# The first stage of a five-stage kernel, reordered: loads by use on four semaphores, diagonals on ScalarE, normalisation in two pieces

## The chip, the cores and the metric

The kernel runs on one core of one Trainium2 chip. Its time is the device time of one execution in microseconds (us); three executions of the kernel before gave 1887.2, 1889.8 and 1894.68 us, median 1889.8. The engines are named as in the profile: PE is TensorE, DVE is VectorE, ACT is ScalarE, POOL is GpSimd, SP is SyncE, which here only issues DMAs.

## The reference, cut to what matters

Two transformer-like layers with modulation, all in float32, on x of 8 sequences of 512 tokens with 128 features. The first stage, which the change rewrites, computes what stands before the scan:

```python
mod = (_silu(L0_c) @ L0_wmod).reshape(L0_c.shape[0], 6, 1, -1)        # the same for layer 1
ga = (2 * (ga >= 0) - 1) * jnp.maximum(jnp.abs(ga), 0.25)              # the gates' bounds, 4 of them in all
h = _layernorm(x, axis=-1) * (1 + ca) + sa
x_sub = h[:, ::2]                                                      # every second token
x_sub = x_sub * jax.lax.rsqrt(jnp.mean(jnp.square(x_sub), axis=-1, keepdims=True) + EPS) * g_norm
xz = jnp.einsum('bld,ed->ble', x_sub, w_in) + b_in
x_proj, gate = jnp.split(xz, 2, axis=-1)                               # silu(gate) is applied to the scan's output
c_sum = Cm.sum(axis=0)

def step(h, xt):                                                       # 256 steps, one after the other
    h = jnp.tanh(h * A + xt[:, :, None] * Bm)
    y = h @ c_sum + Dv * xt
    return (h, y)
```

After it come the scan, an expert layer with 8 experts, attention with relative positions, and a second, routed expert layer, whose outputs are gathered token by token and added to x.

## The kernel before, in words

The program is a row of stages, each a block with one instruction stream for each engine; a stage begins when all engines have ended the one before. The first stage is `prologue`. Its tokens are laid 128 to a tile: x has 32 tiles of 128x128, and the stage needs the 16 even ones (NC). The projections take 512 tokens at a time (BLK), so there are 4 blocks (NBK).

In `prologue` before the change:

- SP issues 12 DMAs: cT, wmod, the whole of x (2 MB), then nine small ones. x counts on the semaphore x_in, the eleven others on w_in, and ACT and PE begin with a wait for all eleven (ALL_W).
- ACT takes a tanh of cT, PE forms the column sums of Cm (into csum, by DVE) and four products with wmod (mod), which ACT copies out of PSUM.
- POOL waits for csum and writes diagC with one instruction: 64 diagonal matrices of 128x128, one per state, each the identity times one column of csum. The scan's PE products take diagC as their weights. A 65th is the identity times Dv.
- DVE scales winT and woT, adds 1 to four parts of mod, bounds the four gates (four instructions each), and only then waits for x and normalises all 16 tiles: moments, root, 16 subtract-and-scale, scale, shift, square, reduce, second root, and a last product. Roots are taken by ACT (`Roots`: DVE writes the argument, ACT takes a square root, DVE refines the reciprocal).
- PE turns the 16 tiles (transposes, 4 to a PSUM bank), ACT copies each bank out (h0T), PE makes two products per block, and ACT writes xp, the raw gate and its tanh (gth) for each; DVE joins the gate's two parts.

Within an engine the order is that of the code; nothing reorders it. Between engines there are only the semaphores. In the scan that follows, each step is a chain between DVE and ACT with a length that the first stage doesn't touch. In the last stage, `experts1`, POOL gathers two rows per token tile k with indirect DMAs, counted on NGOT semaphores in turn; before those of tile k it waits until those of tile k - NGOT have landed.

Of the kernel before, what the change touches and what calls it, by code (L numbers as in the profile page):

```python
# [5 lines left out]
ALU = mybir.AluOpType  # L6
# [92 lines left out]
def layer_norm(dve, v, chain, roots, src, out, n, stats, mv, rstd, tmp, scale, shift):  # L99

    moments(v, chain, src, n, stats, mv)
    roots.rsqrt(dve, v, chain, mv[:, 0:n, 1], rstd[:, 0:n], tmp[:, 0:n])
    for k in range(n):
        chain.add(v.tensor_scalar(out[:, k, :], src[:, k, :], mv[:, k, 0:1], rstd[:, k:k + 1],
                                  ALU.subtract, ALU.mult))
    chain.wait()
    chain(v.tensor_tensor(out[:, 0:n, :], out[:, 0:n, :], scale.unsqueeze(1).to_broadcast([P, n, P]), ALU.mult))
    chain(v.tensor_tensor(out[:, 0:n, :], out[:, 0:n, :], shift.unsqueeze(1).to_broadcast([P, n, P]), ALU.add))


def prologue(nc, d, keep, scan):

    x, mod, ident, ones = keep["x"], keep["mod"], keep["ident"], keep["ones"]
    with ExitStack() as ctx:
# [31 lines left out]
        NBK = NC * P // BLK  # L146
        block = ctx.enter_context(nc.Block())

        @block.sync
        def _(sp):  # L150
            sp.dma_start(cT[:, :, :], d["cT"]).then_inc(w_in, 16)
            sp.dma_start(wmod[:, :, :], d["wmod"]).then_inc(w_in, 16)
            sp.dma_start(x[:, :, :], d["x"]).then_inc(x_in, 16)
            for dst, src in ((winT[:, :], d["w_inT"]), (binc[:, :], d["b_in"]), (gn[:, :], d["g_norm"]),
                             (cm[:, :], d["Cm"]), (am[:, :], d["A"]), (scan["Bm"][:, :], d["Bm"]),
                             (scan["Dv"][:, :], d["Dv"]), (scan["woT"][:, :], d["w_outT"]),
                             (scan["bo"][:, :], d["b_out"])):
                sp.dma_start(dst, src).then_inc(w_in, 16)

        ALL_W = 16 * 11  # L160

        @block.gpsimd
        def _(pool):
            nc.gpsimd.memset(ident[:, :], 0.0).then_inc(zero, 1)
            nc.gpsimd.memset(ones[:, :], 1.0).then_inc(id_ready, 1)
            pool.wait_ge(zero, 1)
# [10 lines left out]
            nc.gpsimd.tensor_tensor(scan["diagC"][:, NS, :], ident[:, :], scan["Dv"][:, 0:1].to_broadcast([P, P]),  # L177
                                    ALU.mult).then_inc(scan_set, 1)
            pool.wait_ge(scan_set, 3)

        @block.scalar
        def _(act):
            act.wait_ge(w_in, ALL_W)
            nc.scalar.activation(cth[:, :, :], cT[:, :, :], ACT.Tanh, scale=0.5).then_inc(c_tanh, 1)
            for n, (lo, hi) in enumerate(((0, 512), (512, 768)) * 2):
                act.wait_ge(mod_ps, n + 1)
                nc.scalar.copy(mod[:, n // 2, lo:hi], pm[n][:, 0:hi - lo]).then_inc(mod_sb, 1)
            roots.serve(act, nc, rstd[:, :], rtmp[:, :])
            roots.serve(act, nc, rstd[:, :], rtmp[:, :])
            for j in range(NBK):  # L190
                act.wait_ge(hT_ps, j + 1)
                nc.scalar.copy(hT[:, j * BLK:(j + 1) * BLK], pm[4 + j % 2][:, :]).then_inc(hT_sb, 1)
            for j in range(NBK):
                act.wait_ge(proj_ps, 2 * j + 1)
                nc.scalar.activation(scan["xp"][:, j * BLK:(j + 1) * BLK], pm[2 * (j % 2)][:, :], ACT.Identity,
                                     bias=binc[:, 0:1]).then_inc(proj_sb, 1)
# [3 lines left out]
                nc.scalar.activation(gate[:, j % 2, :], pm[2 * (j % 2) + 1][:, :], ACT.Identity,  # L200
                                     bias=binc[:, 1:2]).then_inc(proj_sb, 1)
                act.wait_ge(w_scaled, 1)
                nc.scalar.activation(gth[:, j % 2, :], pm[2 * (j % 2) + 1][:, :], ACT.Tanh,
                                     bias=binh[:, 0:1], scale=0.5).then_inc(gate_sb, 1)

        @block.vector
        def _(dve):
            v = nc.vector
            chain = Chain(dve, v_chain)
            dve.wait_ge(c_tanh, 1)  # L210

            chain(v.scalar_tensor_tensor(cth[:, :, :], cth[:, :, :], 1.0, cT[:, :, :], ALU.add, ALU.mult))
            for l in range(2):
                v.tensor_scalar(crep[:, l, :, :], cth[:, l, :].unsqueeze(1).to_broadcast([P, U, NB]), 0.5, None,
                                ALU.mult).then_inc(c_rep, 1)
            chain(v.tensor_scalar(winT[:, :], winT[:, :], gn[:, 0:1], None, ALU.mult))
# [17 lines left out]
            dve.wait_ge(x_in, 16)  # L234

            layer_norm(dve, v, chain, roots, x[:, :, :].rearrange("p (c o) e -> p c o e", o=2)[:, :, 0, :], h, NC,
                       stats, mv, rstd, rtmp, mod[:, 0, P:2 * P], mod[:, 0, 0:P])
            chain(v.tensor_tensor(sq[:, :, :], h[:, :, :], h[:, :, :], ALU.mult))
            chain(v.tensor_reduce(ms[:, :], sq[:, :, :], AX.X, ALU.add))
            chain(v.tensor_scalar(ms[:, :], ms[:, :], 1.0 / P, RMS_EPS, ALU.mult, ALU.add))  # L240
            roots.rsqrt(dve, v, chain, ms[:, :], rstd[:, :], rtmp[:, :])
            v.tensor_tensor(h[:, :, :], h[:, :, :], rstd[:, :].unsqueeze(2).to_broadcast([P, NC, P]),
                            ALU.mult).then_inc(h_ready, 1)
            for j in range(NBK):
                dve.wait_ge(gate_sb, j + 1)

                v.scalar_tensor_tensor(scan["gate"][:, j * BLK:(j + 1) * BLK], gth[:, j % 2, :], 1.0,
                                       gate[:, j % 2, :], ALU.add, ALU.mult).then_inc(gate_used, 1)

        @block.tensor  # L250
        def _(pe):
            mm = nc.tensor.matmul
            pe.wait_ge(w_in, ALL_W)
            pe.wait_ge(id_ready, 2)
# [1578 lines left out]
```

## Time and profile before

| | us |
|---|---|
| median of three executions | 1889.8 |
| lowest, highest | 1887.2, 1894.68 |
| the profiled execution's own time | 1888.83 |
| its span, first to last instruction | 1887.1 |
| first instruction of the scan stage (POOL, after the barrier) | 73.92 |
| last instruction of the first stage (DVE, the fourth gate), end | 73.60 |

The page puts PE at 79% of the span, DVE at 70%, ACT at 48%, POOL at 32%; these are means over stages of different kinds. The first stage takes 73.9 of the 1887.1 us. A row of the timeline reads: start in us, duration in us, engine, line of the code, operation, what it writes and reads, how many were merged into the row, and in brackets how long the engine sat idle before it and what released it. The granted TensorE clock was 0.874 of full speed over the span.

### The profile page before, as it was taken

What the parts mean: (1) busy time and instruction counts of PE and PEld (TensorE: products, weight loads), DVE (VectorE), ACT (ScalarE), POOL (GpSimd) and SP (SyncE); (2) the same over time, 40 slices, a digit from 0 to 9 for tenths busy, and PEclk for the clock granted to TensorE, in tenths of its full rate; (3) what the DMA queues carried; (4) which work ended last, traced back from release to release, by engine and by line L of the source; (5) the groups of instructions that cost most, each with busy time, mean ns of one, the idle gap of its engine ahead of it and who ended that gap; (6) DMA issues with size and microseconds to landing.
All of it is one profiled execution on the core that took longest, in us unless ns stands there. A gap on an engine that the chain in (4) does not pass through costs nothing. (4 is left out here: it accounts for less than half of the span.)

```text
span 1887.1 us, 41774 instructions
## 1 busy us (share of the span) xinstructions
PE 1487.2 (79%) x15118; PEld 1007.2 (53%) x15118; DVE 1326.4 (70%) x3609; ACT 908.8 (48%) x2099; POOL 612.6 (32%) x586
## 2 busy tenths in 40 slices
PE   1277777767699399999999999999999395298490
PEld 0177766766554245555555555555555363187370
DVE  6699999999559636666666666666666674177385
ACT  1455555555121226666666666666666122065250
POOL 3496666662103325111111111111110317502414
PEclk7688888888789799999999999999999777599695
DMA  1400000000000012111111111111110001258342
GB/s 68 118 12 1 1 1 1 1 1 1 12 1 1 17 17 35 28 29 29 28 29 30 29 29 30 29 30 30 30 25 8 15 1 56 65 150 224 94 135 78
DMA packets 146373, 71.54 MB, mean 38 GB/s; under 512 B 95218, under 2 KB 131588, under 8 KB 146052
## 3 DMA queue, kind: packets, MB, share of 16 engines
q1 hardware_dynamic: 141508, 60.62, 14.6%
q0 software_dynamic: 4096, 8.40, 1.5%
q8 instruction: 107, 1.75, 0.4%
q14 instruction: 86, 0.70, 0.1%
q10 hardware_dynamic: 576, 0.07, 0.0%
HBM read 38.11 MB, written 18.35 MB: 30 GB/s over the span
## 5 line engine op out<-in xcount | busy, mean ns | idle before, releaser
L1190 DVE TENSOR_REDUCE ntop<-score 128x1 f32<-128x512 f32 x512 | 318.1, 683 | 253.0 <-PE score L1071 252.9
L1149 ACT ACTIVATE prob<-score,ntop 128x512 f32<-128x512 f32 x512 | 317.6, 687 | 270.0 <-DVE ntop L1190 269.9
L391 ACT ACTIVATE hist<-zp 128x168 f32<-128x168 f32 (+1 forms) x768 | 224.1, 313 | 171.6 <-DVE zp L359 170.9
L1107 PE MATMUL turned<-ident,prob 128*128 128x128 f32 x2048 | 268.5, 280 | 1.5 <-DVE probT L1133 1.5
L441 PEld LDWEIGHTS py<-hist,diagC 128*128 128x128 f32 x2048 | 262.7, 214 | 0.0
L441 PE MATMUL py<-hist,diagC 128*128 128x128 f32 x2048 | 262.5, 297 | 0.0
L1071 PE MATMUL score<-ks,qs 64*128 64x512 f32 x1024 | 257.5, 622 | 0.0
L1107 PEld LDWEIGHTS turned<-ident,prob 128*128 128x128 f32 x2048 | 218.9, 141 | 49.4 <-issue 28.7
L411 POOL TENSOR_TENSOR xb<-xc,Bm 128x1024 f32<-128x1024 f32 x128 | 244.7, 1950 | 1.3
L354 DVE TENSOR_TENSOR gp<-hist,Ap 128x168 f32<-128x168 f32 (+1 forms) x768 | 231.0, 331 | 14.9 <-POOL xb L411 14.9
L359 DVE TENSOR_TENSOR zp<-gp,xb 128x168 f32<-128x168 f32 (+1 forms) x768 | 234.6, 336 | 0.0
L836 POOL TENSOR_TENSOR qr<-rel_q,own_shift 128x256 f32<-128x256 f32 x64 | 37.2, 613 | 549.3 <-DMA key_q<-q_sb 549.3
L1133 ACT COPY probT<-turned 128x512 f32<-128x512 f32 x384 | 198.4, 594 | 1.2 <-PE turned L1107 1.2
L1071 PEld LDWEIGHTS score<-ks,qs 64*128 64x128 f32 x1024 | 89.1, 188 | 169.0 <-issue 169.0
L1091 PEld LDWEIGHTS mixed<-probT,vh 128*16 128x16 f32 x4096 | 100.7, 96 | 95.8 <-issue 95.8
L1067 PE MATMUL score<-tb,qr 32*32 32x512 f32 x4096 | 148.1, 600 | 4.0 <-PEq L850 3.9
L1091 PE MATMUL mixed<-probT,vh 128*16 128x128 f32 x4096 | 136.4, 274 | 0.7 <-issue 0.7
L1449 POOL DMA_INDIRECT got<-sorted_y,pos x64 | 61.1, 954 | 169.3 <-DMA sorted_y<-ysb 150.4
L1177 DVE RECIPROCAL inv<-cm 128x256 f32<-128x256 f32 x64 | 111.5, 1742 | 0.0
L842 POOL TENSOR_TENSOR qs<-key_q,own_batch 128x256 f32<-128x256 f32 x128 | 95.5, 787 | 0.0
L1133 DVE COPY probT<-turned 128x512 f32<-128x512 f32 x128 | 88.5, 691 | 0.1
L1440 POOL DMA_INDIRECT sorted_h<-hz,pos x64 | 63.2, 987 | 48.9 <-DVE pos L1573 29.7
(299 smaller groups left out, 1652.8 us busy)
## 6 DMA issues: line engine op xcount, KB each, us to landing
w<-in_ew SPq DMA_DIRECT2D x46, 320.0 KB
tb<-in_table SPq DMA_DIRECT2D x64, 127.1 KB
sorted_h<-nought SPq DMA_DIRECT2D x2, 2944.0 KB, 17.1
xs<-sorted_h SPq DMA_DIRECT2D x46, 128.0 KB
sorted_y<-ysb SPq DMA_DIRECT2D x46, 128.0 KB
rel_q<-q_sb SPq DMA_DIRECT2D x256, 8.0 KB
ks<-k_sb SPq DMA_DIRECT2D x32, 128.0 KB
key_q<-q_sb SPq DMA_DIRECT2D x248, 8.0 KB
```

The lines of the kernel that those rows point to most:

```text
L354: v.tensor_tensor(g[:, lo:hi], prev[:, lo:hi], Ap[:, lo:hi], ALU.mult).then_inc(decayed, 1)
L359: v.tensor_tensor(zp[j][:, 0:hi - lo], g[:, lo:hi], xb[:, par, u, lo:hi], ALU.add)\
L391: nc.scalar.activation(hist[:, par, u, lo:hi], zp[j][:, 0:hi - lo], ACT.Tanh)\
L411: nc.gpsimd.tensor_tensor(xb[:, par, u:u + XB_STEPS, :].rearrange("p u (s b) -> p u s b", b=NB), xc[:, par, u * NB:(u + XB_STEPS) * NB].re ...
L441: last = mm(py[par][:, 0:P], diagC[:, s, :], hist[:, par, :, s * NB:(s + 1) * NB], start=False, stop=(s == NS - 1))
L1067: mm(score_ps[r][32 * w:32 * w + 32, :], qr[p][rows, w, g, :, :].rearrange("p b v -> p (b v)"), tb[p][rows, s:s + SEQ], start=True, stop=F ...
L1071: mm(score_ps[r][:, :], qs[p][rows, r % 2, g, :, :, :].rearrange("p w b v -> p (w b v)"), ks[p][rows, :], start=False, stop=True).then_inc ...
L1091: last = mm(mixed_ps[32 * c:32 * c + SUMS, bh * P:(bh + 1) * P], vh[:, p, j, b, :], probT[G // 2 % 2][:, j, :, :].rearrange("p t (w b v) - ...
L1107: last = nc.tensor.transpose(turned_ps[BANK[e]][:, j * P:(j + 1) * P], prob[G % 2][e][:, j * P:(j + 1) * P], ident[:, :])
L1133: copy(probT[G // 2 % 2][:, :, G % 2 * GRP + TURN[e], :], turned_ps[BANK[e]][:, :].rearrange("p (j t) -> p j t", j=JT))\
L1149: nc.scalar.activation(prob[G % 2][e][:, :], score_ps[r][:, :], ACT.Exp, bias=ntop[:, G % 2, e:e + 1]).then_inc(prob_ready, 1)
L1190: v.tensor_reduce(ntop[:, G % 2, e:e + 1], score_ps[r][:, :], AX.X, ALU.max, negate=True)\
```

## The change

The first stage is written in another order, and the last one counts its gathers on 4 semaphores in place of 8.

- Loads: cm and cT go first on c_in, then wmod on wmod_in, then only the even tiles of x on x_in (16 pieces of 512 bytes per partition), then the eight small ones and last the odd tiles of x on w_in.
- diagC is written by ACT with 65 instructions, each a Copy of the identity with a column of csum (or Dv) as its scale, in five groups of 12, 20, 12, 20 and 1 between its other work; POOL writes the two constants and a zero only.
- DVE begins the moments behind x_in. Normalisation after the first root goes in two pieces of 8 tiles; between them it scales winT and binh. The gates' bounds, woT and A come after the second piece and the first two joined gates.
- PE turns and projects blocks 0 and 1 behind the first piece, blocks 2 and 3 behind the second. ACT's square root for the second piece stands between its work on blocks 0 and 1.
- In `experts1` NGOT is 4.

```diff
@@ prologue, loads
+            sp.dma_start(cm[:, :], d["Cm"]).then_inc(c_in, 16)
+            sp.dma_start(cT[:, :, :], d["cT"]).then_inc(c_in, 16)
+            sp.dma_start(wmod[:, :, :], d["wmod"]).then_inc(wmod_in, 16)
+            sp.dma_start(by_use(x[:, :, :])[:, :, 0, :], by_use(d["x"])[:, :, 0, :]).then_inc(x_in, 16)
             for dst, src in ((winT[:, :], d["w_inT"]), (binc[:, :], d["b_in"]), (gn[:, :], d["g_norm"]),
...
+                             (by_use(x[:, :, :])[:, :, 1, :], by_use(d["x"])[:, :, 1, :])):
                 sp.dma_start(dst, src).then_inc(w_in, 16)
@@ gpsimd
-            nc.gpsimd.tensor_tensor(scan["diagC"][:, 0:NS, :], ident[:, :].unsqueeze(1).to_broadcast([P, NS, P]),
-                                    csum[:, :].unsqueeze(2).to_broadcast([P, NS, P]), ALU.mult).then_inc(scan_set, 1)
@@ scalar
+            def diagonals(lo, hi):
+                for s in range(lo, hi):
+                    A.activation(scan["diagC"][:, s, :], ident[:, :], ACT.Copy, scale=csum[:, s:s + 1])
...
+            act.wait_ge(c_in, 32)
+            A.activation(cth[:, :, :], cT[:, :, :], ACT.Tanh, scale=0.5).then_inc(c_tanh, 1)
+            act.wait_ge(id_ready, 3)
+            act.wait_ge(csum_sb, 1)
+            diagonals(0, 12)
+            for n, (lo, hi) in enumerate(((0, 512), (512, 768)) * 2):
+                act.wait_ge(mod_ps, n + 1)
+                A.copy(mod[:, n // 2, lo:hi], pm[n][:, 0:hi - lo]).then_inc(mod_sb, 1)
+            roots.serve(act, nc, rstd[:, :], rtmp[:, :])
+            diagonals(12, 32)
+            roots.serve(act, nc, rrms[:, 0:PER], rtmp[:, 0:PER])
+            diagonals(32, 44)
+            act.wait_ge(w_in, ALL_W)
+            for j in range(BLKS):
+                columns(j)
+            act.wait_ge(w_scaled, 1)
+            projected(0)
+            roots.serve(act, nc, rrms[:, PER:NC], rtmp[:, PER:NC])
+            projected(1)
+            for j in range(BLKS, NBK):
+                columns(j)
+            diagonals(44, NS)
+            A.activation(scan["diagC"][:, NS, :], ident[:, :], ACT.Copy, scale=scan["Dv"][:, 0:1]).then_inc(scan_set, 1)
+            for j in range(BLKS, NBK):
+                projected(j)
@@ vector
+            dve.wait_ge(x_in, 16)
+            xe = by_use(x[:, :, :])[:, :, 0, :]
+            moments(v, chain, xe, NC, stats, mv)
+            roots.rsqrt(dve, v, chain, mv[:, :, 1], rstd[:, :], rtmp[:, :])
+            dve.wait_ge(mod_sb, 1)
+            scale, shift = mod[:, 0, P:2 * P], mod[:, 0, 0:P]
+            chain(v.tensor_scalar(scale, scale, 1.0, None, ALU.add))
+            def piece(i):
+                ts = slice(i * PER, (i + 1) * PER)
+                wide = lambda t: t.unsqueeze(1).to_broadcast([P, PER, P])
+                for k in range(i * PER, (i + 1) * PER):
+                    chain.add(v.tensor_scalar(h[:, k, :], xe[:, k, :], mv[:, k, 0:1], rstd[:, k:k + 1],
+                                              ALU.subtract, ALU.mult))
+                chain.wait()
+                chain(v.tensor_tensor(h[:, ts, :], h[:, ts, :], wide(scale), ALU.mult))
+                chain(v.tensor_tensor(h[:, ts, :], h[:, ts, :], wide(shift), ALU.add))
+                chain(v.tensor_tensor(sq[:, ts, :], h[:, ts, :], h[:, ts, :], ALU.mult))
+                chain(v.tensor_reduce(ms[:, ts], sq[:, ts, :], AX.X, ALU.add))
+                chain(v.tensor_scalar(ms[:, ts], ms[:, ts], 1.0 / P, RMS_EPS, ALU.mult, ALU.add))
+                roots.rsqrt(dve, v, chain, ms[:, ts], rrms[:, ts], rtmp[:, ts])
+                v.tensor_tensor(h[:, ts, :], h[:, ts, :], rrms[:, ts].unsqueeze(2).to_broadcast([P, PER, P]),
+                                ALU.mult).then_inc(h_ready, 1)
...
+            piece(0)
+            dve.wait_ge(w_in, ALL_W)
             chain(v.tensor_scalar(winT[:, :], winT[:, :], gn[:, 0:1], None, ALU.mult))
+            v.tensor_scalar(binh[:, :], binc[:, 1:2], 0.5, None, ALU.mult).then_inc(w_scaled, 1)
+            piece(1)
+            gated(0)
+            gated(1)
             chain(v.tensor_scalar(scan["woT"][:, :], scan["woT"][:, :], 0.5, None, ALU.mult))
...
@@ tensor
+            for i in range(PIECES):
+                for j in range(i * BLKS, (i + 1) * BLKS):
+                    turned(j)
+                for j in range(i * BLKS, (i + 1) * BLKS):
+                    projected(j)
@@ experts1
-    NW, NX, NY, NGOT = 5, 4, 4, 8
+    NW, NX, NY, NGOT = 5, 4, 4, 4
```

How the orders move, in three places. First DVE, at the start of the moments (L91). Before, the last of the four gates' bounds (guard) stood ahead of them:

```order
L230 TENSOR_SCALAR guard<-mod 128x128
L231 SCALAR_TENSOR_TENSOR guard<-mod 128x128
L232 TENSOR_SCALAR guard<-guard 128x128
L233 SCALAR_TENSOR_TENSOR mod<-guard 128x128
L91 BN_STATS stats<-x 128x6 x16
L94 BN_AGGR mv<-stats 128x2 x16
L96 TENSOR_SCALAR mv<-mv 128x16
L74 TENSOR_SCALAR rtmp<-mv 128x16
```

The same engine in the changed kernel, from its first instruction that does work:

```order
L226 COPY csum<-pm 128x64
L229 SCALAR_TENSOR_TENSOR cth<-cth,cT 128x16
L231 TENSOR_SCALAR crep<-cth 128x128 x2
L91 BN_STATS stats<-x 128x6 x16
L94 BN_AGGR mv<-stats 128x2 x16
L96 TENSOR_SCALAR mv<-mv 128x16
L74 TENSOR_SCALAR rtmp<-mv 128x16
```

Of the instructions on mod, the gates, winT, woT and A none is left ahead of the moments: one (1 added to the scale) stands behind the first root, the others behind the first piece or later.

Second ACT, from the square roots (rstd, rrms) to the first two blocks' tanh (gth). Before:

```order
L85 ACT_TABLE_LOAD
L85 ACTIVATE rstd<-rtmp 128x16 x2
L192 COPY h0T<-pm 128x512 x4
L195 ACTIVATE xp<-pm,binc 128x512
L200 ACTIVATE gate<-pm,binc 128x512
L203 ACT_TABLE_LOAD
L203 ACTIVATE gth<-pm,binh 128x512
L195 ACTIVATE xp<-pm,binc 128x512
```

ACT in the changed kernel, from the third group of diagonals:

```order
L176 ACTIVATE diagC<-ident,csum 128x128 x12
L180 COPY h0T<-pm 128x512 x2
L184 ACTIVATE xp<-pm,binc 128x512
L189 ACTIVATE gate<-pm,binc 128x512
L191 ACT_TABLE_LOAD
L191 ACTIVATE gth<-pm,binh 128x512
L85 ACT_TABLE_LOAD
L85 ACTIVATE rrms<-rtmp 128x8
L184 ACTIVATE xp<-pm,binc 128x512
L189 ACTIVATE gate<-pm,binc 128x512
L191 ACT_TABLE_LOAD
L191 ACTIVATE gth<-pm,binh 128x512
```

The second piece's root now stands between two tanhs, with a table load before and after it.

Third ACT at the end of the stage. Before, the last two blocks followed one another:

```order
L195 ACTIVATE xp<-pm,binc 128x512
L200 ACTIVATE gate<-pm,binc 128x512
L203 ACTIVATE gth<-pm,binh 128x512
L195 ACTIVATE xp<-pm,binc 128x512
L200 ACTIVATE gate<-pm,binc 128x512
L203 ACTIVATE gth<-pm,binh 128x512
```

The end of the stage on ACT in the changed kernel, from the copies of blocks 2 and 3 (h0T):

```order
L180 COPY h0T<-pm 128x512 x2
L176 ACTIVATE diagC<-ident,csum 128x128 x20
L216 ACTIVATE diagC<-ident,Dv 128x128
L184 ACTIVATE xp<-pm,binc 128x512
L189 ACTIVATE gate<-pm,binc 128x512
L191 ACTIVATE gth<-pm,binh 128x512
L184 ACTIVATE xp<-pm,binc 128x512
L189 ACTIVATE gate<-pm,binc 128x512
L191 ACTIVATE gth<-pm,binh 128x512
```

21 diagonals now stand between the copies and the last two blocks.

## Rows read from the trace of the kernel before

**Rows 1.** Busy time by stretch: us, busy us (instructions) by engine, clock, DMA, GB/s.

```profile
core 0: us, PE busy (x) PEld busy (x) DVE busy (x) ACT busy (x) POOL busy (x), PEclk, DMA share, GB/s
18.30:29.10 10.80, 0.00 (x0) 0.00 (x0) 10.77 (x2) 1.26 (x1) 10.73 (x2) 0.58 0.00 0
...
34.40:58.20 23.80, 0.00 (x0) 0.00 (x0) 22.58 (x67) 0.43 (x2) 0.00 (x0) 0.50 0.00 0
```

**Rows 2.** Timeline, the load of x and the first work behind the loads.

```profile
1.74 0.43 SPq L153 DMA_DIRECT2D x<-in_x  x1
...
12.51 0.22 ACT L184 ACTIVATE cth<-cT 128x16 f32<-128x16 f32 x1 [10.41 <-DMA bo<-in_b_out]
```

**Rows 3.** DMA view: x's landing; then 6-10, 10-12.3 and 78-90 us.

```profile
x<-in_x SPq DMA_DIRECT2D x1, 2048.0 KB, 9.0
...
DMA packets 106, 1.60 MB, mean 399 GB/s; under 512 B 3, under 2 KB 9, under 8 KB 9
...
DMA packets 1161, 0.29 MB, mean 127 GB/s; under 512 B 910, under 2 KB 1161, under 8 KB 1161
...
DMA packets 6767, 3.46 MB, mean 289 GB/s; under 512 B 16, under 2 KB 6766, under 8 KB 6766
```

**Rows 4.** Timeline, 12.5 to 34.4 us: modulation, diagonals, gates' bounds.

```profile
13.39 4.40 PE L258 MATMUL pm<-wmod,crep 128*128 128x512 f32 x8 [0.17 <-DVE crep L214]
...
14.79 13.88 POOL L174 TENSOR_TENSOR diagC<-ident,csum 128x8192 f32<-128x8192 f32 x1 [12.78 <-DVE csum L222]
...
18.29 10.82 DVE L226 TENSOR_SCALAR mod<-mod 128x128 f32<-128x128 f32 x2 [3.65 <-ACT mod L187]
...
34.04 0.29 DVE L233 SCALAR_TENSOR_TENSOR mod<-guard 128x128 f32<-128x128 f32 x1
```

**Rows 5.** Timeline, 34.4 to 58.2 us: normalisation.

```profile
34.37 3.19 DVE L91 BATCH_NORM_STATS2 stats<-x 128x6 f32<-128x128 f32 x16
...
39.22 0.21 ACT L85 ACTIVATE rstd<-rtmp 128x16 f32<-128x16 f32 x1 [19.66 <-DVE rtmp L74]
...
40.59 4.19 DVE L104 TENSOR_SCALAR h<-x,mv,rstd 128x128 f32<-128x128 f32 x16
...
54.11 0.17 DVE L240 TENSOR_SCALAR ms<-ms 128x16 f32<-128x16 f32 x1
...
55.90 2.29 DVE L242 TENSOR_TENSOR h<-h,rstd 128x2048 f32<-128x2048 f32 x1
```

**Rows 6.** Timeline, 58.2 to 73.6 us: transposes, projections, gates.

```profile
58.25 3.76 PE L265 MATMUL pm<-ident,h 128*128 128x128 f32 x16 [40.46 <-DVE h L242]
...
60.26 0.58 ACT L192 COPY h0T<-pm 128x512 f32<-128x512 f32 x1 [0.27 <-PE pm L265]
...
65.70 1.28 ACT L203 ACT_TABLE_LOAD   x1
66.99 0.69 ACT L203 ACTIVATE gth<-pm,binh 128x512 f32<-128x512 f32 x1
...
69.28 0.70 ACT L195 ACTIVATE xp<-pm,binc 128x512 f32<-128x512 f32 x1
...
72.91 0.69 DVE L247 SCALAR_TENSOR_TENSOR gate<-gth,gate 128x512 f32<-128x512 f32 x1 [1.04 <-ACT gth L203]
```

**Rows 7.** Prices elsewhere: groups by form (DVE, ACT), then timeline of eight ACT.

```profile
L354 DVE TENSOR_TENSOR gp<-hist,Ap 128x168 f32<-128x168 f32 (+1 forms) x768 | 231.0, 331 | 14.9 <-POOL xb L411 14.9
...
L670 ACT COPY acc<-px 128x128 f32<-128x128 f32 x32 | 6.9, 269 | 58.3 <-PE px L742 58.3
...
1509.72 3.19 ACT L537 ACTIVATE hz<-x,offsetz,rstdz 128x128 f32<-128x128 f32 x8 [1.54 <-DVE offsetz L501]
```

**Rows 8.** End: last gather, data moved 1868 to 1872 us (40 slices), last combining.

```profile
1867.85 0.94 POOL L1449 DMA_INDIRECT got<-sorted_y,pos  x1 [0.30 <-issue]
...
GB/s 0 0 246 164 246 0 0 0 0 0 0 0 0 0 0 287 287 82 0 0 0 0 0 0 0 0 0 0 0 0 0 0 0 0 0 0 0 0 0 0
...
1880.17 3.06 DVE L1629 SCALAR_TENSOR_TENSOR acc<-got,wt,acc 128x128 f32<-128x128 f32 x8
```

More of the change, by code:

```diff
@@ L96, in moments @@
     chain(v.tensor_scalar(mv[:, 0:n, 1], mv[:, 0:n, 1], LN_EPS, None, ALU.add))
[L99 to L108, printed above, removed]
 def prologue(nc, d, keep, scan):
     x, mod, ident, ones = keep["x"], keep["mod"], keep["ident"], keep["ones"]
+    PIECES = 2
+    PER = NC // PIECES
     with ExitStack() as ctx:
@@ L185, in _ @@
[L185 to L190, printed above, removed]
+            A = nc.scalar
+            def diagonals(lo, hi):
+                for s in range(lo, hi):
+                    A.activation(scan["diagC"][:, s, :], ident[:, :], ACT.Copy, scale=csum[:, s:s + 1])
@@ L191, in _, with columns, projected @@
+            def columns(j):
                 act.wait_ge(hT_ps, j + 1)
[L192 to L193 removed]
+                A.copy(hT[:, j * BLK:(j + 1) * BLK], pm[4 + j % 2][:, :]).then_inc(hT_sb, 1)
+            def projected(j):
                 act.wait_ge(proj_ps, 2 * j + 1)
[L195 to L196 removed]
+                A.activation(scan["xp"][:, j * BLK:(j + 1) * BLK], pm[2 * (j % 2)][:, :], ACT.Identity,
+                             bias=binc[:, 0:1]).then_inc(proj_sb, 1)
@@ L199, in _ @@
                     act.wait_ge(gate_used, j - 1)
[L200 to L204, printed above, removed]
+                A.activation(gate[:, j % 2, :], pm[2 * (j % 2) + 1][:, :], ACT.Identity,
+                             bias=binc[:, 1:2]).then_inc(proj_sb, 1)
+                A.activation(gth[:, j % 2, :], pm[2 * (j % 2) + 1][:, :], ACT.Tanh,
+                             bias=binh[:, 0:1], scale=0.5).then_inc(gate_sb, 1)
+            act.wait_ge(c_in, 32)
[23 more added lines that the diff above has]
+                projected(j)
+            act.wait_ge(scan_set, 1)
         @block.vector
@@ L233, in _ @@
                     chain(v.scalar_tensor_tensor(g, guard[:, 0, :], -1.0, guard[:, 1, :], ALU.add, ALU.mult))
[L234 to L248, printed above, removed]
+            for j in range(BLKS, NBK):
+                gated(j)
         @block.tensor
@@ L252, in _, with turned @@
             mm = nc.tensor.matmul
-            pe.wait_ge(w_in, ALL_W)
-            pe.wait_ge(id_ready, 2)
-            mm(pm[7][:, 0:NS], ones[:, :], cm[:, :], start=True, stop=True).then_inc(csum_ps, 1)
-            pe.wait_ge(c_rep, 2)
-            for n, (lo, hi) in enumerate(((0, 512), (512, 768)) * 2):
-                mm(pm[n][:, 0:hi - lo], crep[:, n // 2, :, :].rearrange("p u b -> p (u b)"),
-                   wmod[:, n // 2, lo:hi], start=True, stop=True).then_inc(mod_ps, 1)
-            pe.wait_ge(h_ready, 1)
-            for j in range(NBK):
+            def turned(j):
+                pe.wait_ge(h_ready, j // BLKS + 1)
                 if j >= 2:
@@ L266, in _, with projected @@
                 last.then_inc(hT_ps, 1)
-            for j in range(NBK):
+            def projected(j):
                 pe.wait_ge(hT_sb, j + 1)
```

50 lines of the change are left out of this document (29 added, 21 removed).

## The prediction

> **What bounds the kernel now.** I read the busy time by stretch first, then the timeline of the first stage, and then only as much of the last stage as the gathers need. The code between is the same in both kernels, and the scan's first instruction waits for a barrier of all engines at 73.9 us, so the question is when the first stage's last instruction ends. Before, that is the fourth joined gate, at 72.91 + 0.69 = 73.6 us [rows 6].
>
> The stage is one chain with four parts. Nothing but DMAs runs until 12.5: ACT's first tanh is released by the last load to land [rows 2]. From 12.5 to 34.4 comes work that normalisation doesn't need, and in it the striking row: DVE's two additions on 128x128 tiles take 10.82 us, while POOL's single product for diagC runs from 14.79 to 28.67 [rows 4]. Both engines are busy for the whole stretch of 10.8 us, and DVE does two instructions in it [rows 1]. The reader is to see that a busy DVE there is a held DVE. From 34.4 to 58.2 DVE alone works (22.6 of 23.8 us) and PE nothing [rows 1]; then PE, ACT and DVE take turns until 73.6 [rows 6]. So DVE's start on the moments, at 34.37 [rows 5], hangs on all loads, on POOL and on the gates' bounds, and on nothing that the moments use: x itself landed at 1.74 + 9.0 = 10.7 [rows 2, 3].
>
> **The change, part by part.** I build the new stage forward in time from the span's start.
>
> *The even half of x.* x is 2.10 MB and in long packets moved at 399 GB/s [rows 3], so 5.3 us, which puts its start at about 5.5. Ahead of it now stands cm too, 32 KB of 256-byte rows, at 127 GB/s [rows 3] 0.3 us: 5.8. The half is 1.05 MB, but in pieces of 512 bytes. Packets of that size went at 289 GB/s in a store [rows 3]: 3.6 us, landing at 9.4. Bounds: 399 GB/s gives 8.4, and 127 GB/s, the rate of the still smaller ones, gives 14.1. I take 9.4, by the row of equal size. The odd half and the small loads follow it, by the same rates until about 16; nothing waits for them before 26.
>
> *Early ACT and PE work* costs nothing. wmod lands at about 5.5, PE's eight products take 4.4 [rows 4], so the copies of mod end near 10.3. Twelve diagonals lie ahead of those copies, in time when ACT has nothing else. The root is first asked for 4.8 us after the moments begin (34.37 to 39.22 [rows 5]), at 14.2. Slack 2.5 us and more with the table load.
>
> *Moments, root, scale:* 40.59 - 34.37 = 6.2 [rows 5], and one addition of 0.3: 15.9. POOL has no product any more, so nothing holds DVE.
>
> *A piece.* Eight subtractions are half of 4.19, 2.1. Five passes of 1024 elements: a pass of 2048 takes 2.29 [rows 5] and one of 168 takes 0.33 [rows 7], so 1024 takes 1.22, with the gap 1.26, in all 6.3. The mean and the root are 55.90 - 54.11 = 1.8 [rows 5]. Sum 10.2. The first piece ends at 26.1. In whole, two pieces are 20.4 where one pass of all 16 tiles was 17.6 (40.59 to 58.19): splitting costs 2.8 us of DVE. winT and binh I put at 0.3 each, like an instruction of the gates' bounds (0.29 [rows 4]); the second piece starts at 26.7 and, if its root is served at once, ends at 36.9.
>
> *ACT between.* 65 diagonals are new on ACT. No row shows a Copy of 128 columns with one pointer for its scale, from SBUF. A copy without one takes 0.27, and two ACTIVATEs in a row overlap: six with 0.70 each end 3.6 after the first starts [rows 6], 0.6 each, so 0.17 is the lower end. Eight of 128 columns with two pointers took 3.19 [rows 7], 0.40 each, the upper end. I take 0.29, half way. The Trainium skill (ScalarE: Activation LUTs, section What ACT_TABLE_LOAD costs) has this price: 186 ns, 0.833 ns per element and 93 ns per pointer, less 93 ns of overlap; that would be 0.293 each, an estimate by the page. Twenty lie between the roots: 14.4 to 20.2 (22.4 at 0.40), and the next root is asked for at 23.5. Twelve more end at 27.2; PE's first bank is turned at 26.1 + 1.1 (16 transposes take 3.76 with waits [rows 6]), 27.2. Level, so an ACT slower than this is late here.
>
> *The second root.* Before, the first gth began at 66.99, 8.7 after the transposes did, with four banks turned ahead of the first product [rows 6]. With two banks it is half of 3.76 less, 6.8: it ends at 26.1 + 6.8 + 0.7 = 33.6, and the next table load (1.28) at 34.9. DVE asks for the root at 26.7 + 2.1 + 4 x 1.26 + 0.4 = 34.2: with ACT's own steps 0.8 late. The second piece ends at 37.7. The Trainium skill speaks against this (ScalarE: Activation LUTs, section What ACT_TABLE_LOAD costs): it adds some 1.38 us of drain to every switch of tables, which for the two loads on this path would be 2.8 us more, an estimate by that page. The trace disagrees: gth starts 0.01 after its table load ends [rows 6]. I keep 0.8.
>
> *The end.* Transposes and copies of two banks: 60.26 + 0.58 - 58.20 = 2.6 [rows 6], 40.3. The 21 diagonals, the part that I find costly, are on the path now, for DVE waits for gates 2 and 3 only: 21 x 0.29 = 6.1 (3.6 to 8.4), 46.4. Six ACTIVATEs 3.6 and the last gate 0.7 [rows 6]: 50.7. What runs beside: DVE joins two gates by 39.5 and does what I moved there, the bounds with two additions (34.33 less 18.29 + 10.82, 5.2 [rows 4]) and 1.0 for the rest, by 46; gate 2 is asked of it at 48.2. PE's last products (eight instructions took 4.4 [rows 4]) end by 45.
>
> *NGOT 4.* A gather waits for the one 8 issues back, 8 x 1.24 = 10 us, instead of 16 back. The last gather is issued at 1867.85, the last data move at 1869.8 (the second burst, slices 15 to 17 of 0.1 us) [rows 8], 2 us. Nothing by data movement; and the last eight combinings begin at 1880.2, 11 us later, so the tail hangs on DVE. What this row can't show is when the semaphore counts: bounds 0 and the rival below.
>
> The sum: 73.6 - 50.7 = 22.9 us. On its own time, 1888.8, that gives 1865.9; the profiled execution is 1.0 below the median of the runs, so against 1889.8 it is 1866.9. I forecast 1867.
>
> **The rivals.**
>
> *ACT becomes the bound of the stage.* For it: 19 us of new work on an engine that already closes the stage. With 0.40 per diagonal the last group costs 2.3 more, the third ends 1.3 late and pushes the second root by as much: 3.6 us, 1870.5. Beside it, a mechanism of its own: ACT stands idle behind each table load for as long again as the load. Two loads stand on the path to the second root, so twice 1.3 from the row of the load, 2.6 us: 1869.5. Against it, the gap of 0.01 [rows 6]. It is the rule of the Trainium skill named above.
>
> *x comes no earlier than everything else.* 2048 short packets, or a queue that ends its 13 loads together: x_in fires at 14.1 to 15. Then everything moves by 5: 1872. For it: the slow last stretch of the loads (127 GB/s). Against it: 289 GB/s for 512 bytes.
>
> *Slower than before: the gathers' count comes late.* If a gather's semaphore is counted not 2 but L us after its issue, POOL stands still L - 10 us in each of the three rounds of the second half that wait for a gather of that half, and the last gather's own L follows: 1867.9 + 3(L - 10) + L, against 1882.5, when DVE takes the last rows now (the last two of eight from 1880.17). It eats the 22.9 from L = 16.9 on; L = 20 gives 1867.9 + 30 + 20 = 1917.9 for the last rows, 35.4 later than now, in all 1866.9 + 35.4 = 1902: 12 slower. For it: before, POOL waited only for gathers 20 us old, so an unwaited step of 0.94 + 0.30 says only that L is under 20. Against it: data done in 2 us [rows 8].
>
> **How the numbers follow.** The forecast's own case 0.77; ACT as the bound, drains included, 0.09; x late 0.08; gathers 0.03; something in the unchanged stages that moves by some us, 0.03. Below: x at 8.4 (1.0), diagonals at 0.17 (2.5), no late root (0.8) give 1862.6, and the three runs lie up to 2.6 under their median: 1859. Above: the first two rivals together, 3.6 + 5, give 1875.5: 1876. The range is 1859 to 1876. What can be told from no change is 0.5%, 9.4 us. Every case but the gathers' and part of the last is beyond it: faster 0.95, same 0.02, slower 0.03.
>
> **What would show it.** Moments beginning at 9.4 (8.4 to 14.1); POOL idle and no DVE instruction of 128x128 above 0.3 us; the first piece's last product ending at 26.1, the second's at 37.7; 65 diagonals at 0.29 a piece; the second rrms root 0.8 after DVE asks; the scan's first instruction at 51.0; gathers in steps of 1.24 with no wait between. The forecast is wrong if the scan begins after 56, or if it begins at 51 and the time is not within 5 us of 1867, which would put the cause behind the first stage.

## The result, and the profile after

| | before | changed |
|---|---|---|
| median of 4 executions each, us | 1888.5 (1883.44 to 1894.68) | 1865.47 (1855.28 to 1869.98) |
| ratio, 95% interval | | 0.9866 [0.9819, 0.9912] |
| the profiled execution's own time, span | 1888.83, 1887.1 | 1868.96, 1867.2 |
| scan stage's first instruction | 73.92 | 51.78 |

The change made the kernel 1.3% faster. The forecast was 1867, range 1859 to 1876. Between the two profiled executions lie 19.9 us, and 22.1 of them were there when the scan began. Nothing of that was given back in the scan or in attention: at the first scatter of the last stage the lead is 23.8 us. It is 17.4 at the first gather, 20.0 at the 33rd and 19.9 at the end.

The first stage of the changed kernel in the timeline; columns as in [rows 2]. First, up to the end of the first piece:

```profile
2.92 0.22 ACT L195 ACTIVATE cth<-cT 128x16 f32<-128x16 f32 x1 [0.82 <-DMA cT<-in_cT]
...
3.99 3.61 ACT L176 ACTIVATE diagC<-ident,csum 128x128 f32<-128x128 f32 x12 [0.85 <-DVE csum L226]
...
6.57 5.01 PE L318 MATMUL pm<-wmod,crep 128*128 128x512 f32 x8 [2.94 <-DMA wmod<-in_wmod]
...
9.99 3.19 DVE L91 BATCH_NORM_STATS2 stats<-x 128x6 f32<-128x128 f32 x16 [5.62 <-DMA x<-in_x]
...
14.96 5.94 ACT L176 ACTIVATE diagC<-ident,csum 128x128 f32<-128x128 f32 x20
...
16.47 2.14 DVE L246 TENSOR_SCALAR h<-x,mv,rstd 128x128 f32<-128x128 f32 x8
...
25.38 1.23 DVE L255 TENSOR_TENSOR h<-h,rrms 128x1024 f32<-128x1024 f32 x1
```

The reader is to see the bracket behind L91: DVE now waits for x alone, and starts at 9.99 where it started at 34.37 [rows 5]. ACT begins at 2.92, not 12.51 [rows 2], and no DVE row of 128x128 is a held one.

The same view, from the first piece's end to the scan:

```profile
28.57 5.12 PE L309 MATMUL pm<-h0T,winT 128*128 128x512 f32 x8
...
34.02 0.69 ACT L191 ACTIVATE gth<-pm,binh 128x512 f32<-128x512 f32 x1
...
34.38 0.17 DVE L74 TENSOR_SCALAR rtmp<-ms 128x8 f32<-128x8 f32 x1
34.72 1.28 ACT L85 ACT_TABLE_LOAD   x1
36.02 0.21 ACT L85 ACTIVATE rrms<-rtmp 128x8 f32<-128x8 f32 x1
...
36.26 0.20 DVE L76 RECIPROCAL rrms<-rrms 128x8 f32<-128x8 f32 x1 [1.71 <-ACT rrms L85]
...
37.30 1.23 DVE L255 TENSOR_TENSOR h<-h,rrms 128x1024 f32<-128x1024 f32 x1
...
41.07 5.95 ACT L176 ACTIVATE diagC<-ident,csum 128x128 f32<-128x128 f32 x20
...
46.92 0.39 ACT L216 ACTIVATE diagC<-ident,Dv 128x128 f32<-128x128 f32 x1
47.21 0.67 ACT L184 ACTIVATE xp<-pm,binc 128x512 f32<-128x512 f32 x1
...
50.77 0.69 DVE L261 SCALAR_TENSOR_TENSOR gate<-gth,gate 128x512 f32<-128x512 f32 x1 [0.96 <-ACT gth L191]
51.78 0.29 POOL L457 COPY xc<-xp 128x128 f32<-128x128 f32 x1 [49.63 <-POOLq L104]
```

Two things on ACT set the end. The second piece's root is asked for at 34.38 + 0.17 and comes at 36.02, behind the tanh and a table load, so DVE sits idle 1.71 us where a root served at once costs 0.28. And 21 diagonals hold back blocks 2 and 3 from 41.07 to 47.21.

Busy time by stretch, the view of [rows 1]:

```profile
9.90:26.70 16.80, 1.68 (x4) 0.54 (x2) 15.46 (x61) 10.81 (x34) 0.00 (x0) 0.63 0.25 68
26.70:38.50 11.80, 6.94 (x16) 3.60 (x16) 9.68 (x23) 9.37 (x15) 0.00 (x0) 0.79 0.00 1
38.50:51.50 13.00, 6.14 (x16) 3.36 (x16) 8.11 (x26) 11.61 (x31) 0.00 (x0) 0.76 0.00 0
```

DVE bounds the first stretch (15.46 of 16.80), no engine the second alone, and ACT the third (11.61 of 13.00): the bound of the stage moved from DVE to ACT.

### The profile page after: what moved, and what is told of

It reads as the page before. It is cut to its first block and busy times, and to the rows that moved or that the text cites. A ratio compares the mean times of both kernels' runs of the same rounds, so it can differ in the third digit from the quotient of the medians.

```text
span 1867.2 us, 41862 instructions
## 1 busy us (share of the span) xinstructions
PE 1491.4 (80%) x15118; PEld 1010.8 (54%) x15118; DVE 1317.8 (71%) x3621; ACT 930.6 (50%) x2167; POOL 598.7 (32%) x584
## 5 line engine op out<-in xcount | busy, mean ns | idle before, releaser
L403 DVE TENSOR_TENSOR gp<-hist,Ap 128x168 f32<-128x168 f32 (+1 forms) x768 | 231.1, 331 | 14.7 <-POOL xb L460 14.7
```

The lines of the kernel that those rows point to most:

```text
L403: v.tensor_tensor(g[:, lo:hi], prev[:, lo:hi], Ap[:, lo:hi], ALU.mult).then_inc(decayed, 1)
```

## The experiments

The scan's first instruction is the measure for edits to the first stage; why, the last section says. How far it repeats, traces of the same first stage show: the changed kernel's began the scan at 51.78, 51.79 (e5) and 51.50 (e10), the one before at 73.92 and 72.69 (e6). One execution each unless more are given. e1 to e4 ran on one chip, beside "before" at 1876.8 (one execution), e5 to e8 on a second, beside 1882.57 (median of 11, 1874.72 to 1894.3), and the last three on a third. The question of the first four was which part of the change brought what, and what POOL's product really held.

**e1, the kernel before with the gates' bounds behind normalisation.**

```diff
+            chain(v.tensor_scalar(mod[:, 0, P:2 * P], mod[:, 0, P:2 * P], 1.0, None, ALU.add))
             chain(v.tensor_scalar(winT[:, :], winT[:, :], gn[:, 0:1], None, ALU.mult))
...
+            dve.wait_ge(x_in, 16)
+            layer_norm(...)        # then woT, A, the other additions and the bounds
```

> The kernel before with one edit: DVE does only the csum copy, the scale's addition, winT and binh ahead of the moments, and the gates' bounds, woT and A behind normalisation, where DVE waits for gates anyway. Loads and POOL's diagC as before. Read: start of the scan (73.9 us before). Theory A, POOL's product holds every DVE instruction: moments begin near 28.7 instead of 34.4, the scan at 68.2. Theory B, it holds only DVE instructions of some kinds (tensor_scalar on a large tile among them) and lets the moments' instructions through: the moments begin near 17 while POOL works, the subtractions at 28.7 instead of 40.6, the scan at about 62. If the bounds don't fit into DVE's idle time, either is later by up to 5.

1872.11 us; the scan began at 66.81, 7.1 earlier than before. The timeline of this kernel:

```profile
13.32 13.88 POOL L174 TENSOR_TENSOR diagC<-ident,csum 128x8192 f32<-128x8192 f32 x1 [11.31 <-DVE csum L217]
...
15.80 11.48 DVE L219 TENSOR_SCALAR mod<-mod 128x128 f32<-128x128 f32 x1 [2.63 <-ACT mod L187]
...
27.81 3.18 DVE L91 BATCH_NORM_STATS2 stats<-x 128x6 f32<-128x128 f32 x16
```

The first addition is held until POOL ends, and the moments behind it with it. Of the 7.1 us, 1.5 come from POOL starting earlier (13.32 for 14.79 [rows 4]). The times are near those of theory A (27.8 for 28.7, 66.8 for 68.2), but that doesn't decide between the theories: whether the moments themselves would be held stayed open, since a held instruction stood in front of them.

**e2, the kernel before with the diagonals on ACT**, 30 ahead of the first root and 35 behind it.

```diff
-            nc.gpsimd.tensor_tensor(scan["diagC"][:, 0:NS, :], ...)
+            for s in range(30):
+                nc.scalar.activation(scan["diagC"][:, s, :], ident[:, :], ACT.Copy, scale=csum[:, s:s + 1])
             roots.serve(act, nc, rstd[:, :], rtmp[:, :])
+            for s in range(30, NS): ...
```

> The kernel before with one edit: the 65 diagonals by ACT, 30 ahead of the first root and 35 between the two roots, where ACT is idle; POOL's products are gone. Loads and DVE's order as before. Read: start of the scan (73.9 us before). My theory: DVE's two additions take 0.5 instead of 10.8 us, ACT's 65 x 0.30 us = 19.3 are hidden, and the scan starts at 63.6. Rival: DVE was not held by POOL but by something else at that place, and the scan stays at 73.9.

1875.77 us; the scan began at 63.38, 10.5 earlier.

```profile
18.17 0.49 DVE L228 TENSOR_SCALAR mod<-mod 128x128 f32<-128x128 f32 x2 [3.40 <-ACT mod L180]
...
23.92 3.19 DVE L91 BATCH_NORM_STATS2 stats<-x 128x6 f32<-128x128 f32 x16
```

The two additions that took 10.82 [rows 4] take 0.49. What held DVE was POOL's product and nothing else, and taking it off POOL is worth 10.5 us here, by itself.

**e3, the changed kernel with normalisation in one piece.**

```diff
-    PIECES = 2
+    PIECES = 1
```

> The changed kernel with PIECES = 1: all 16 tiles normalised in one piece, then all transposes and projections as before the change; the diagonals stay in ACT's five groups. Read: start of the scan (51.8 us in the changed kernel). My theory: two pieces cost DVE 2.8 us and a late root 1.5, and give back the transposes and products of two blocks; by the old rows 16.5 + 17.6 + 0.5 = 34.6 for the last product, 14.7 to the last gth, 6.3 for the 21 diagonals, 0.7 for the last gate: 56.3, so the scan at 56.6, 4.8 later. Rival: the split gives nothing, because what it overlaps comes back as 2.8 + 1.5 and waits: the scan within 1 us of 51.8.

1860.08 us; the scan began at 54.53, 2.8 later than in the changed kernel. I had expected 4.8.

```profile
37.58 3.62 PE L305 MATMUL pm<-h0T,winT 128*128 128x512 f32 x8
```

Of the 2.0 us missing, 0.8 is the last product of normalisation, which ended at 33.8 and not 34.6. Most of the rest is PE: its first eight products took 3.62 at a granted clock of 1.00 (2.4 GHz), where they took 5.12 at 0.72 in the changed kernel and 4.87 at 0.74 before, both of which run their first products at 0.50 (1.2 GHz). Splitting pays, though it gives DVE more work (2.8 us by the prediction's working).

**e4, the changed kernel with diagC by POOL again.**

```diff
+            pool.wait_ge(csum_sb, 1)
+            nc.gpsimd.tensor_tensor(scan["diagC"][:, 0:NS, :], ...)
@@ scalar
-            diagonals(...)          # all five groups
```

> The changed kernel with diagC by POOL again, as one product behind csum (ready at 3.9 us) and the small one for Dv behind the loads; ACT makes no diagonals. Read: start of the scan (51.8 us in the changed kernel) and what DVE does until 18. POOL's product runs from 4 to 18. Theory A, it holds every DVE instruction: the moments start at 18, 8 us late, ACT's last 21 diagonals (6.2) and its lateness (1.5) are gone: scan at 52. Theory B, the moments pass (10 to 14.6) and the subtractions wait until 18, 1.5 us late: the scan at 45.6 to 47.6, where DVE's own gates' bounds, which end at 46.2 now, are the next bound.

1864.83 us; the scan began at 58.33, 6.5 later than in the changed kernel.

```profile
4.08 14.04 DVE L232 TENSOR_SCALAR crep<-cth 128x128 f32<-128x128 f32 x2
4.12 13.92 POOL L169 TENSOR_TENSOR diagC<-ident,csum 128x8192 f32<-128x8192 f32 x1 [1.97 <-DVE csum L227]
...
18.05 1.05 DVE L91 BATCH_NORM_STATS2 stats<-x 128x6 f32<-128x128 f32 x5
...
18.18 1.22 PE L319 MATMUL pm<-wmod,crep 128*128 128x512 f32 x1 [14.47 <-DVE crep L232]
```

Neither theory's time came out, because the product caught crep, which both had forgotten: PE waited for it until 18.18, and mod with it. The experiment was badly placed; e9 mends it.

**e9, the same with csum copied behind crep**, so that POOL starts after it.

```diff
-            dve.wait_ge(csum_ps, 1)
-            v.tensor_copy(csum[:, :], pm[7][:, 0:NS]).then_inc(csum_sb, 1)
             dve.wait_ge(c_tanh, 1)
...
+            dve.wait_ge(csum_ps, 1)
+            v.tensor_copy(csum[:, :], pm[7][:, 0:NS]).then_inc(csum_sb, 1)
             dve.wait_ge(x_in, 16)
```

> The kernel of e4 (diagC by POOL as one product) with one move: DVE's csum copy stands behind cth and crep, so that the moments are the first DVE instructions beside POOL's product, and not crep, which in e4 took 14.04 us. In e1 and e4 a tensor_scalar was first in the row and everything behind it came late with it, so they can't tell which kinds of DVE instruction POOL's product holds. Theory A, every kind: moments at 18.0 as in e4, the scan at 56 to 58. Theory B, only some: moments at 9.7 to 10.4 while POOL works, and a later instruction (the small additions, the root's steps with two inputs, or the scale's addition) shows the long time and ends at 18; then the subtractions begin at 18.3 to 19.5 instead of 16.5, ACT has no diagonals at the end (6.2 us less), and the scan starts at 47.5 to 49.

1769.18 us; the scan began at 51.20, where the changed kernel on the same chip (e10) has 51.50. Its timeline:

```profile
4.11 13.88 POOL L169 TENSOR_TENSOR diagC<-ident,csum 128x8192 f32<-128x8192 f32 x1 [1.96 <-DVE csum L233]
...
9.80 3.19 DVE L91 BATCH_NORM_STATS2 stats<-x 128x6 f32<-128x128 f32 x16 [5.85 <-DMA x<-in_x]
...
13.03 1.17 DVE L94 BATCH_NORM_AGGREGATE mv<-stats 128x2 f32<-128x6 f32 x16
...
14.24 3.79 DVE L96 TENSOR_SCALAR mv<-mv 128x16 f32<-128x16 f32 x1
...
45.45 0.69 ACT L191 ACTIVATE xp<-pm,binc 128x512 f32<-128x512 f32 x1 [0.91 <-PE pm L310]
...
49.59 1.29 DVE L262 SCALAR_TENSOR_TENSOR gate<-gth,gate 128x512 f32<-128x512 f32 x2
```

In the middle of POOL's 13.88 us the moments run at their usual 3.19 and 1.17. The next instruction, an addition on 16 columns that takes 0.18 in the changed kernel, takes 3.79 and ends with POOL. So the hold goes by the kind of instruction, not by its size, and the theory that the moments pass is right on that. Its time was not. The scan's 47.5 to 49 assumed that the subtractions start by 19.5, and they start at 20.04. From there to the scan it took 31.2 us, 2.0 more than in the changed kernel's first trace without its 21 diagonals (35.3 less 6.1). ACT, with no diagonals before them, stands 0.91 for PE's products of block 2; and DVE ends the gates' bounds only at 49.56, behind ACT's last tanh (49.31), and joins the last two gates together in 1.29, where one took 0.69. Diagonals on ACT are as good, and they need no such placing.

The Trainium skill (SBUF — State Buffer, section SBUF: two separate sides) says that the port pair that DVE and GpSimd share is locked for a whole instruction, and that DVE takes it in a perf mode that uses two ports, or, against a GpSimd instruction that reads SBUF, with two inputs in SBUF. The trace fits the lock: the addition waits for the whole of POOL's product (3.79 for 0.18), the moments for nothing. In which mode the addition ran the trace doesn't show.

**e5, the changed kernel with NGOT 1**, every pair of gathers waiting for the pair before; the test of the slower rival.

```diff
-    NW, NX, NY, NGOT = 5, 4, 4, 4
+    NW, NX, NY, NGOT = 5, 4, 4, 1
```

> The changed kernel with NGOT = 1: each token's two gathers wait until the two of the token before are counted. It measures L, the time from a gather's issue to its count. With L = 2 us, as the moved data show, POOL's step per token grows from 2.5 to 3.2 us, the last gather goes from 1848 to about 1860 and the time by 0 to 3 us. The slower rival of the prediction, L of 17 to 20: a step per token of 18 to 21, and the time longer by some 250 us.

1867.95 us, within the changed kernel's own spread. POOL's rows near the end, and DVE's last combining:

```profile
1791.92 0.94 POOL L1498 DMA_INDIRECT got<-sorted_y,pos  x1 [2.34 <-DMA got<-sorted_y,pos]
...
1853.95 1.03 POOL L1498 DMA_INDIRECT got<-sorted_y,pos  x1 [1.82 <-DMA got<-sorted_y,pos]
1855.29 0.94 POOL L1498 DMA_INDIRECT got<-sorted_y,pos  x1 [0.31 <-issue]
...
1858.05 0.74 DVE L1678 SCALAR_TENSOR_TENSOR acc<-got,wt,acc 128x128 f32<-128x128 f32 x2 [3.49 <-DMA got<-sorted_y,pos]
```

Each pair now waits, 1.7 to 2.3 us in the second half, and the last gather is issued at 1855.3. These waits do set the pace at the end: DVE stands up to 3.5 us for each pair, 51.4 us in all. The time is the same only because the experts' work ended far earlier. From the first gather to ACT's last copy out of PSUM (L1545) it took 71.0 us, where the changed kernel took 138.7. Busy time by stretch for these, first the changed kernel, then this one:

```profile
1715.00:1854.00 139.00, 73.32 (x348) 58.23 (x346) 76.61 (x205) 44.15 (x116) 61.80 (x64) 0.73 0.43 119
1712.00:1783.00 71.00, 67.41 (x348) 54.12 (x346) 63.36 (x171) 43.71 (x115) 27.01 (x28) 0.98 0.67 185
```

PE and ACT do the same instructions in half the time, and ACT's waits of up to 20.7 us, which the last section shows, are absent. e1 to e4 and e6 to e8, with NGOT 8 or 4, took 128 to 137 for it, the last three of them on the chip of e5. So how closely the gathers follow one another moved the experts' work by far more than anything in the first stage, and the slow gathers behind it ate all of that again. It is one execution, and an NGOT of 2 or 3 was not run.

**e6, the kernel before with NGOT 4.**

```diff
-    NW, NX, NY, NGOT = 5, 4, 4, 8
+    NW, NX, NY, NGOT = 5, 4, 4, 4
```

> The kernel before with NGOT = 4 and nothing else: the change's part in the last stage alone. My theory: steps of 1.24 us between gathers as before, none of them waiting, the time the same within the runs' own spread (1883 to 1895). Rival: a wait appears in some gather, the last gather is later.

1875.05 us, inside the spread of before. Within each half all gathers stood 0.30 us apart, without a wait for one another. Going from 8 to 4 does nothing.

**e7, the changed kernel with the whole of x in one load.**

```diff
-            sp.dma_start(by_use(x[:, :, :])[:, :, 0, :], by_use(d["x"])[:, :, 0, :]).then_inc(x_in, 16)
+            sp.dma_start(x[:, :, :], d["x"]).then_inc(x_in, 16)
```

> The changed kernel with the whole of x loaded in the place of its even half, in long packets, and no odd half at the end. Read: start of the moments (9.99 us in the changed kernel) and of the scan (51.8). 2.10 MB at 399 GB/s take 5.3 us behind wmod: moments at 11 to 11.5, scan at 53, 1.2 later: halving x bought little, since its short packets are slower. Rival: short packets cost so much that the whole x is no later: moments at 10 or before.

1859.15 us; moments at 10.95, 1.0 later, scan at 52.38, 0.6 later. The DMA view from 6 to 10 us, the changed kernel:

```profile
DMA packets 2642, 1.16 MB, mean 290 GB/s; under 512 B 605, under 2 KB 2642, under 8 KB 2642
```

and this one:

```profile
DMA packets 107, 1.75 MB, mean 438 GB/s; under 512 B 0, under 2 KB 0, under 8 KB 0
```

So half the bytes in short packets were there 1.0 us sooner than all of them in long ones. The second root then kept DVE 1.33 us in place of 1.71, so 0.6 reached the scan. Both are one trace against one: with the loads of the changed kernel the moments began between 9.68 and 10.41, which makes the gain 0.5 to 1.3.

**e8, a version that should beat both**: ACT serves the second root before the tanh of blocks 0 and 1, and more diagonals lie where ACT is idle (14, 29, 11, 4, 6 and 1).

```diff
+            diagonals(54, 58)
             projected(0)
-            roots.serve(act, nc, rrms[:, PER:NC], rtmp[:, PER:NC])
             projected(1)
+            roots.serve(act, nc, rrms[:, PER:NC], rtmp[:, PER:NC])
+            bent(0)
+            bent(1)
...
-            diagonals(44, NS)
+            diagonals(58, NS)
```

> The changed kernel with two edits on ACT: the second piece's root is served before the tanh of blocks 0 and 1 (both tanhs behind it under one table load), and diagonals are moved from the end into ACT's idle time (groups of 14, 29, 11, 4 and 6 + 1 in place of 12, 20, 12, 20 + 1). Root on time (1.5 us), 14 diagonals fewer on the path at the end (4.2 us): ACT would end the stage at 45.8, DVE, which has its gates' bounds until 46 and then two gates to join, at 46.4 to 47.6. Scan at 47 to 48.3 instead of 51.8, time 1861 to 1862 against 1865.5. Rival: PE's products for blocks 2 and 3, slow at their clock, end at 43.5 and bound it no later than that: no change to the numbers; or ACT's longer first groups delay the copies of mod and the first root: scan at 49 or later.

1856.41 us, median of 6 (1849.06 to 1867.15); ratio to before 0.9855 [0.9815, 0.9895]. The scan began at 46.95, 4.8 earlier than in the changed kernel.

```profile
35.74 0.20 DVE L76 RECIPROCAL rrms<-rrms 128x8 f32<-128x8 f32 x1 [0.78 <-ACT rrms L85]
...
39.72 1.87 ACT L176 ACTIVATE diagC<-ident,csum 128x128 f32<-128x128 f32 x6
...
44.63 0.71 ACT L193 ACTIVATE gth<-pm,binh 128x512 f32<-128x512 f32 x1
...
45.01 0.29 DVE L290 SCALAR_TENSOR_TENSOR mod<-guard 128x128 f32<-128x128 f32 x1
...
45.34 1.29 DVE L267 SCALAR_TENSOR_TENSOR gate<-gth,gate 128x512 f32<-128x512 f32 x2
```

The root costs 0.78 in place of 1.71, and only seven diagonals stand at the end. Now the gates' bounds on DVE end at 45.3, level with ACT's last tanh, and the last two gates are joined behind both.

**e10 and e11, the changed kernel and e8 again, side by side.** No edit; these and e9 ran on another chip, beside "before" at 1787.9 (median of 13, 1782.65 to 1802.26).

> The changed kernel once more, with rounds, on the same chip and beside the same runs of before as e11, so that e11 and it can be compared. Stage times as in its first profile (moments at 10, scan at 51.8); the time within its runs so far, 1855 to 1870.

> The kernel of e8 once more, with rounds, beside e10. Its first stage ended 4.8 us before the changed kernel's (scan at 47.0 against 51.8). If that is passed on whole, the medians of e11 and e10 differ by 4.8; the last stage alone scatters by some 10 us from run to run, so a difference of 0 to 10 would not be against it.

The changed kernel took 1769.38 (median of 8, 1766.92 to 1779.06), ratio to before 0.9904 [0.9871, 0.9936]; the other version 1760.06 (median of 5, 1757.74 to 1766.23), 0.9853 [0.9816, 0.9891]. That is 9.3 us between the two, and all executions of the one lie below all of the other. The scan's start (51.50 and 46.00) accounts for 5.5; the rest arose behind it, where kernels scatter. On the chip of e8 the gain over the changed kernel isn't shown in the whole time: its ratio to before, 0.9855, lies with the 0.9866 of the first result.

## Why the prediction was right

| step | forecast | measured |
|---|---|---|
| moments begin | 9.4 | 9.99 |
| subtractions of the first piece begin | 15.9 | 16.47 |
| first piece ends | 26.1 | 26.61 |
| a diagonal on ACT | 0.29 | 0.30 (5.94 / 20) |
| second root late by | 0.8 | 1.4 (1.71 less 0.28) |
| second piece ends | 37.7 | 38.53 |
| 21 diagonals at the end | 6.1, to 46.4 | 6.1, to 47.21 |
| last gate ends | 50.7 | 51.46 |
| scan begins | 51.0 | 51.78 |
| total, own time of the profiled execution | 1865.9 | 1868.96 |
| total, median of the runs | 1866.9 | 1865.47 |

**What was in the way before.** I read the two additions of 10.82 us as held by POOL. e2 shows it: with the product gone they take 0.49, and the scan begins 10.5 us earlier. The moments begin 24.4 us earlier than before in all, and the rows of before divide that up, for they stood in one line ahead of the moments. From 34.37 back to 29.11 are 5.3 us of gates' bounds, back to 18.29 the two additions with the hold (10.8 [rows 4]), back to 12.51 [rows 2] DVE's work on crep, winT, woT, A and csum and its wait for mod (5.8), and from there to 9.99 the loads, 2.5. The loads are thus the smallest share, and of their 2.5 us e7 puts 1.0 on taking half of x.

**The loads.** The rate for short packets was right, 290 GB/s (a quarter of the packets are under 512 bytes) for the 289 that I took from a store. The moments of kernels with the same loads began between 9.68 and 10.41, so 9.4 was a little early. The rival that x comes with everything else is dead.

**ACT.** The disputed price came out at 0.30. The rule of the Trainium skill (ScalarE: Activation LUTs, section What ACT_TABLE_LOAD costs) gave 0.293, and the trace agrees. Of the drain that the same section puts behind a table load there is nothing: the root begins 0.02 us after its load ends, so the rival built on it is dead too, and so is ACT at 0.40 a diagonal.

**The second root** was the term that was mis-sized, 1.4 for 0.8. The transposes began 0.65 later than forecast, and ACT's tanh 7.3 us after them, where I had halved to 6.8: the turns of two banks took 1.8 and not 1.7, and the gate's copy came 3.45 us after the first product began, at a granted clock of 0.58, where the rows of before that I drew on have 3.19 at 0.60. DVE asked only 0.35 later than forecast. The two together, 0.35 and 0.6, make the 0.8 us by which the second piece and all behind it are later, to within 0.15; the group of diagonals and what follows it took the time that I gave them.

**The gathers.** The slower rival needed a count that comes 16.9 us or more behind a gather. With NGOT 1 the wait shows it directly: 1.7 to 2.3 us behind the end of the second gather's issue in the second half, some 2.8 from its start (0.94 + 1.8), and up to 5 while weights stream. NGOT of 4 waits for a gather 10 us old. It never waits, and neither did 8. So the step from 8 to 4 costs nothing, as forecast (e6). The gathers as such are not free: spaced out in e5, they let the experts' work end 68 us sooner.

**What lay outside.** 22.1 us at the scan became 19.9 at the end. The stages up to the last kept the lead in these two traces (23.8 at the first scatter), but they too scatter: from the scan's start to the first scatter all kernels took 1476 to 1482 us. The last stage took 4 us more than before's. That the sum came so near the median is partly luck: executions of the changed kernel alone lie 14.7 us apart.

## What to carry to other kernels

An engine that the profile shows busy for 10 us with two small instructions is held, not busy: look for the long instruction beside it (here POOL's, beside DVE), and move that one, since which instructions are held depends on their kind. When a stage is one chain, order loads, waits and instructions by what the chain needs first, and then fill the engine that serves it (here ACT) only where it would be idle: 14 of the 21 diagonals left at the end and one tanh ahead of a root were worth 4.8 us more. An edit that leaves the time as it was can still have moved much inside a stage: compare stretches, not only ends (e5). Judge an edit of some us by the time at which the next stage begins, when the rest of the kernel scatters by more than the edit.

## What was not expected of the hardware

**The last stage scatters, and differs by chip.** With the same code but for NGOT, from the first scatter to the span's end took 331.0 us before, 334.9 in the changed kernel, and 322.9 to 334.1 in e1 to e8, in no order that their edits would give. On the chip of e9 to e11 every kernel was 90 to 100 us faster than in all runs before. Each chip was used at one time only, so chip and time can't be told apart; I say chip. The first scatter of the changed kernel came at the same time, 1532.38 for 1532.30; the difference lies behind it. Busy time by stretch of the changed kernel from there to the first gather, in the first profile:

```profile
1532.00:1716.00 184.00, 120.82 (x558) 94.70 (x559) 91.32 (x240) 68.83 (x182) 63.20 (x65) 0.77 0.41 113
```

and on the chip of e10:

```profile
1532.00:1657.00 125.00, 110.05 (x556) 88.44 (x557) 91.99 (x239) 68.67 (x180) 64.05 (x65) 0.95 0.58 165
```

The instructions are the same, and DVE, ACT and POOL are busy as long; PE is granted 0.77 in place of 0.95, and the data move at 113 in place of 165 GB/s. The waits in the last stage of the first profile have rows that e10 lacks:

```profile
ACT acc L1545 <- remote: 79.4, 6, 20.7
ACT l L1528 <- remote: 25.9, 4, 10.5
ACT g L1522 <- remote: 24.5, 4, 10.8
```

ACT stood up to 20.7 us at a time for something that this core's trace doesn't show. Nearly all of this falls where POOL issues indirect DMAs one right behind the other. While the scatters go out (1532 to 1612) ACT is busy 8.9 of 80 us, and 36.7 in e10; in the stretches of the gathers (1716 to 1756, 1808 to 1850) 6.0 of 40 and 4.3 of 42; but 33.0 of 52 between those two. e5, where each pair of gathers waits for the one before, has no such wait from its first gather on, though its scatters, left as they were, have them. So on that chip the stalls go with dense indirect DMAs, and on the chip of e10 dense ones bring none. What joins the two stays open.

**Half of x costs nearly the time of all of it**, when it is cut into 512-byte packets: 290 GB/s for 438 in long ones, so loading only the tiles that are needed first brought some 1.0 us (e7) and not half of the transfer.
